# Rope scores of the last attention layer: made in a stage of their own, or as steps of the layer's own list

## The reference, cut to what matters

```
ckv = x @ Wkv;  kr = rope(ckv @ Wkr);  qr = rope(x @ Wqr)       # kr, qr: 2048 x 64
k, v, q = ckv @ Wkup, ckv @ Wvup, x @ Wq                        # 16 heads of 16
ar = qr @ kr.T                                                  # 2048 x 2048, one for all heads
scores = (q @ k.T + ar) / scale, causal;  out = softmax(scores) @ v @ Wo
```

## Time and profile before

| | |
|---|---|
| median of 3 runs | 2820.98 us |
| profiled execution | 2811.07 us, span 2809.3 us |
| PE busy | 2515.8 us, 90% |
| DVE busy | 1890.8 us, 67% |
| ACT busy | 1232.5 us, 44% |
| mean granted TensorE clock | 0.91 of full |

### The profile page before, as it was taken

The page is one execution under the profiler, slowest core; times in us unless marked ns, Lnnn a source line. Parts: engine busy times, 40 slices in busy tenths (PEclk is TensorE's granted clock), DMA queues, the critical chain, the costliest instruction groups (busy, mean ns, idle before and its releaser), DMA issues.

```text
span 2809.3 us, 38846 instructions
## 1 busy us (share of the span) xinstructions
PE 2515.8 (90%) x14390; PEld 1277.0 (45%) x14390; DVE 1890.8 (67%) x4599; ACT 1232.5 (44%) x1494; POOL 151.6 (5%) x338
## 2 busy tenths in 40 slices
PE   5899989989999998999999999987675999999985
PEld 3543434335555655433333333334333556565654
DVE  6466878844545442888888888764735777776618
ACT  3233656661111112166676667664110355555541
POOL 3100102110000000000000000000000001010100
PEclk9756999999999999599999999899875899999998
DMA  5600303000000004400300300000177326262200
GB/s 193 130 1 1 46 2 47 2 1 19 1 0 1 12 1 160 54 1 2 46 1 1 46 1 1 1 1 16 56 216 194 79 72 115 65 114 68 60 1 30
DMA packets 73905, 130.44 MB, mean 46 GB/s; under 512 B 12530, under 2 KB 31730, under 8 KB 70130
## 3 DMA queue, kind: packets, MB, share of 16 engines
q1 hardware_dynamic: 73716, 127.97, 20.4%
HBM read 88.84 MB, written 38.27 MB: 45 GB/s over the span
## 4 chain that ended last, share of the span: by engine, by line
PE 66%; DVE 21%; DMA 5%; issue 3%; SPq 3%; ACT 2%; POOL 0%; DVEq 0%; ACTq 0%; POOLq 0%
PE PS L971 18%; PE PS L888 15%; PE PS L742 12%; DVE MP L1324 11%; PE PS L748 7%; PE PS L950 7%; PE PS L846 4%; SPq L485 2%; ACT PF L1110 1%; DVE QF L1165 1%; PE PS L896 1%; DVE ST L1158 1%; DMA QR<-MRL 1%; DMA rope_scores<-HT 1%; DMA WA<-rope_scores 1%
## 5 line engine op out<-in xcount | busy, mean ns | idle before, releaser
L1110 ACT ACTIVATE PF<-PS 128x1024 f32<-128x1024 f32 (+3 forms) x1152 | 1055.1, 952 | 879.5 <-PE PS L950 525.7
L1324 DVE TENSOR_REDUCE MP<-PS 128x1 f32<-128x512 f32 (+3 forms) x1664 | 987.8, 652 | 217.2 <-PE PS L888 142.9
L888 PE MATMUL PS<-KR,QR 48*128 48x512 f32 (+3 forms) x2304 | 775.3, 481 | 107.4 <-DVE MP L1324 43.4
L888 PEld LDWEIGHTS PS<-KR,QR 48*128 48x128 f32 x2304 | 354.5, 202 | 652.4 <-DVE MP L1324 473.6
L971 PE MATMUL PS<-PF,VO 128*32 128x512 f32 (+3 forms) x4608 | 606.8, 601 | 0.2
L950 PE MATMUL PS<-QR,KR 50*128 50x512 f32 (+3 forms) x2304 | 510.0, 433 | 27.9 <-DMA QR<-MRL 21.2
L1320 DVE CUSTOM_DVE_ANT_0 JUNK<-PS,WA 128x512 bf16<-128x512 f32 (+3 forms) x512 | 286.5, 605 | 117.6 <-issue 48.9
L950 PEld LDWEIGHTS PS<-QR,KR 50*128 50x128 f32 x2304 | 248.9, 198 | 214.9 <-ACT PF L1110 139.7
L748 PE MATMUL PS<-RQ,RK 64*128 64x512 f32 (+3 forms) x1920 | 260.8, 371 | 0.0
L742 PE MATMUL PS<-HT,WA 128*128 128x512 f32 x512 | 221.1, 592 | 0.0
L696 POOL TENSOR_SCALAR_AFFINE_SELECT PF<-PF 128x256 f32<-128x256 f32 x256 | 103.7, 408 | 2165.4 <-ACT PF L1110 2162.3
(11 more groups left out here) (142 smaller groups left out, 1423.0 us busy)
## 6 DMA issues: line engine op xcount, KB each, us to landing
WA<-rope_scores SPq DMA_DIRECT2D x88, 256.0 KB, 3.2
rope_scores<-HT SPq DMA_DIRECT2D x28, 256.0 KB, 2.5
WC<-rope_scores SPq DMA_DIRECT2D x24, 256.0 KB, 3.2
QR<-parts_a_q SPq DMA_DIRECT2D x18, 256.0 KB, 7.7
KR<-parts_a_k SPq DMA_DIRECT2D x18, 256.0 KB, 10.2
QR<-parts_b_q SPq DMA_DIRECT2D x18, 256.0 KB, 12.8
KR<-parts_b_k SPq DMA_DIRECT2D x18, 256.0 KB, 16.4
QR<-parts_c_q SPq DMA_DIRECT2D x18, 256.0 KB, 7.0
```

The lines of the kernel that those rows point to most:

```text
L888: ins = mm(bank(slots[h][0], w), QR[rows, t0 + tb * P:t0 + (tb + 1) * P], KR[rows, t0 + s0:t0 + s0 + w], start=True, stop=not masked)
L1110: sc.activation(PT[:, u % SETS, 2 * q:2 * q + 2, off:CH], src, ACT.Exp).then_inc(L.exp_done, 1)
L1324: ins = v.reduce_max(MP[:, i, c, y:y + 1], src, AX.X)
```

## The change

The stage `ar` is taken out. A step `("rope", n)` stands in C's own list in front of the maxima of tile n, for group 0 alone, with a planner cost of 1.0 w / 512 + 0.3. It takes one bank of the ring of three: PE makes the three products, DVE moves the bank to `AR[n % 5]`, where the maxima of the next steps read it, waits for its own write (`ar_made`) and frees the bank; SP writes the tile to DRAM. From the sixth tile on DVE waits until the tile that lay in the buffer before is written out. Groups 1 to 3 read the tiles back as before. The first reads come at the end of group 0. SP loads the last rope chunk and the last stack chunk directly behind `p2`, and the stacks of group 1 in three pieces of four DMAs, behind the `pv` steps 0, 5 and 10.

```diff
@@ plan
+            if self.rope and g == 0 and p == 0:
+                ones.append((1.0 * w / CH + 0.3, ("rope", n // NP)))
             ones.append(((1.24 if self.rope else 1.14) * w / CH + (0.34 if self.rope else 0.1), ("max", n)))
-TAKES = {"max": 2, "mtr": 1, "otr": 1}
+TAKES = {"max": 2, "mtr": 1, "otr": 1, "rope": 1}
-                   ("", wave("o1", "hyp", "p2") + each("ar")), ("C", None), ("", wave("o2", "hypout"))]
+                   ("", wave("o1", "hyp", "p2")), ("C", None), ("", wave("o2", "hypout"))]
@@ SP, attention_steps
-                for g in range(2, NG):
+                for g in range(1, NG):
                     for i in range(3):
-                        stacks[(g - 1) * L.n_group - 1 + STACK_STEP * i] = (g, i)
+                        stacks[max(0, (g - 1) * L.n_group - 1) + STACK_STEP * i] = (g, i)
...
-                        if n < n_tiles:
+                        if len(L.tiles) <= n < n_tiles:
                             sp.wait_ge(L.slot_free, ring)
+                            if n - AR_RING < len(L.tiles):
+                                sp.wait_ge(ar_out[n % AR_RING], 16 * (n // AR_RING))
                             settled("sp", sp)
                             ar_load(L, n)
+                    if step[0] == "rope":
+                        n = step[1]
+                        tb, i, s0, w = L.tiles[n]
+                        sp.wait_ge(ar_made, n + 1)
+                        sp.dma_start(scr_ar[tb, :, s0:s0 + w], AR[n % AR_RING][:, 0:w]).then_inc(ar_out[n % AR_RING], 16)
@@ SP, attention
-                if not L.rope:
-                    parts_in_dram(L, NC - 1)
+                parts_in_dram(L, NC - 1)
+                if L.rope:
+                    load_rope(L, NC - 1)
                 load_chunk(L, NC - 1)
...
-                    for i in range(NC):
-                        sp.wait_ge(ar_out[i], 16 * ar_place.count(i))
-                    for n in range(AR_RING):
-                        ar_load(L, n)
-                sp.wait_ge(L.stack_in, NC * STACK_DMAS)
-                load_stacks(L, 1, 1)
@@ PE, attention
+                    if step[0] == "rope":
+                        tb, i, s0, w = L.tiles[step[1]]
+                        if tb % BPC == 0 and i == 0:
+                            pe.wait_ge(L.rope_in, (tb // BPC + 1) * ROPE_DMAS)
+                        for part in range(len(ROPE_PARTS)):
+                            ins = rope_product(bank(slot, w), step[1] % 2, RQ, tb * P, P, RK, s0, w, part)
+                        ins.then_inc(L.slot_ready, 1)
@@ DVE, attention_steps
+                    if step[0] == "rope":
+                        a = step[1]
+                        tb, i, s0, w = L.tiles[a]
+                        if a >= AR_RING:
+                            dve.wait_ge(ar_out[a % AR_RING], 16 * (a // AR_RING))
+                        dst, src = AR[a % AR_RING][:, 0:w], bank(slot, w)
+                        if s0 + w == (tb + 1) * P:
+                            v.tensor_tensor(dst, src, MASK[:, CH - w:CH], ALU.add).then_inc(ar_made, 1)
+                        else:
+                            v.tensor_copy(dst, src).then_inc(ar_made, 1)
+                        dve.wait_ge(ar_made, a + 1)
+                        dve.sem_inc(L.slot_free, 1)
                     if step[0] == "max":
...
-                        if L.rope and p == 0:
-                            dve.wait_ge(ar_in[a % AR_RING], 16 * (a // AR_RING + 1))
+                        if L.rope and p == 0 and g > 0:
+                            dve.wait_ge(ar_in[a % AR_RING], 16 * ((a - len(L.tiles)) // AR_RING + 1))
```

More of the change, by code:

```diff
@@ L309, in build @@
         AR = [WA[:, 4096 + CH * n:4096 + CH * (n + 1)] for n in range(4)] + [WC[:, 1792:2304]]
-        ARS = [HT[:, c].rearrange("p k t -> p (k t)") for c in range(NC)]
         NAT = {"gate": QF[:, 0:2048].rearrange("p (m d) -> p m d", d=D),
@@ L356, in build @@
         x_done = sem("x_done")
-        ar_out = [sem(f"ar_out{i}") for i in range(NC)]
+        ar_made = sem("ar_made")
+        ar_out = [sem(f"ar_out{i}") for i in range(AR_RING)]
         ar_in = [sem(f"ar_in{i}") for i in range(AR_RING)]
@@ L384, in build @@
                  "ffn": (18, 0), "lin": (6, 2), "hyp": (2, 0), "hypout": (2, 0)}
-        ar_banks = lambda c: (BPC * (c + 1), 0)
         D_COUNT, A_COUNT, HT_AT = {}, {}, []
@@ L395, in build @@
                 steps[i] = (k, c, d_total, a_total)
-                d_banks, a_banks = ar_banks(c) if k == "ar" else BANKS[k]
+                d_banks, a_banks = BANKS[k]
                 d_total += d_banks
@@ L408, in build @@
                     NORM_OF[k, c] = len(HT_AT)
[L411 to L414, removed]
         L_KEY = {"a": "A", "b": "B", "c": "C"}
@@ L535, in attention_steps @@
                         if i == 0:
-                            sp.wait_ge(L.pv_done, (g - 1) * L.n_group)
+                            if g > 1:
+                                sp.wait_ge(L.pv_done, (g - 1) * L.n_group)
                             sp.wait_ge(L.stack_in, (g - 1 + NC) * STACK_DMAS)
@@ L549, in load_rope, with attention @@
                         sp.dma_start(dst[HALF * h:HALF * (h + 1), i, t].bitcast(F32), scr_r[w][i, :, t]).then_inc(L.rope_in, 16)
-            def rope_tiles(L, c, d0):
-                if c == 0:
-                    parts_in_dram(L, NC - 1)
+            def attention(L):
+                parts_in_dram(L, NC - 1)
+                if L.rope:
                     load_rope(L, NC - 1)
[L556 to L562, removed]
-                if not L.rope:
-                    parts_in_dram(L, NC - 1)
                 load_chunk(L, NC - 1)
@@ L611, in _ @@
                         project(k, c, d0)
-                    if k == "ar":
-                        rope_tiles(L2, c, d0)
                     if k == "hypout":
@@ L854, in main @@
                     token_major(lambda kk, i: VH[:, kk, blk(i)], lambda kk: OUTW[k][:, kk, :], KD, d_bank, d_ready)
[L855 to L863, removed]
                 if k in ("hyp", "hypout"):
@@ L1244, in main @@
                         v.tensor_copy(NW[:, 6, 0:1], ONE[:]).then_inc(l1w_free, 1)
[L1245 to L1258, removed]
                 if k in ("hyp", "hypout"):
@@ L1300, in attention_steps @@
                 for step in L.steps:
-                    if step[0] in ("mtr", "otr"):
+                    if step[0] in ("mtr", "otr", "rope"):
                         n = ring.next()
@@ L1386, in attention @@
                     dve.wait_ge(a_free, A_COUNT[L_KEY[L.name]])
-                    for i in range(NC):
-                        dve.wait_ge(ar_out[i], 16 * ar_place.count(i))
                 attention_steps(L)
```

## The result

Before 2820.43 us, after 2786.02 us (medians of four runs each): ratio 0.988, interval 0.9848 to 0.9911, 34.4 us less where 27.4 were forecast. Timed again in a second series with more runs of the kernel before, the pair gave 2811.9 and 2791.8 us, ratio 0.9922, interval 0.9899 to 0.9944: some 20 to 22 us. The two series overlap only at the ends of their intervals. A likely reason is that the stages ahead of C vary from run to run: in the changed kernel's profile of the second series the last projection ends at 2108.6 us instead of 2087.6. How much of the difference between the medians that makes is not shown. One place where it shows is the middle of the kernel, at another granted clock.

A forecast was written before the change was run, and what follows sets the result against it. DVE, with the ring of three banks, was taken to pace group 0's maxima, PE all after; 49.4 + 14.7 - 29.7 - 4.0 - 3.0 = 27.4 us gained, 2821.0 - 27.4 = 2793.6 us; forecast's case 2781 to 2805 (0.70).

The forecast's parts named there:

- Start of C: End of p2: DVE starts at about 2090.8 instead of 2140.2, 49.4 us earlier, PE waiting only for p2's last banks.
- The pause: 2152.3 to 2167.0, DVE waiting for a tile read behind stack loads: 14.7 us go, as group 0 reads nothing back.
- Group 1's stacks at nothing: Three load pieces, about 9 us each, hidden by four tiles of slack; without cover up to 5 us a piece.
- DVE waits on the writes: Rival, chance 0.09: each stack piece holds tile writes and row DMAs back, 5 us each, 15 us lost, 2809.
- Rows of chunk 0, 3 us: First score near tile 6: PE waits for chunk 0's row DMAs behind four tile writes, DVE runs dry, 3 us.
- Own wait and increment, 4.0 us: Behind each of 40 moves: DVE's wait for its own write and the semaphore increment, 0.1 us each time.
- Moves at 24.3 / 0.82 = 29.7 us, products covered at nothing: Group 0: 40 moves on DVE, the pacing engine, 82% busy; PE's 25 us of products hidden behind DVE's time.
- The dear bound: All in place, products not covered: 64.1 - 24.3 - 4.0 - 25 - 3 = 7.8 us gained, 2813.
- series: Rival, chance 0.12: with three banks, rope product and move run one after the other in group 0; time 2813.
- The end moves by as much: After group 0's maxima, order and PE's pace stay, so the kernel's end moves as much as theirs.
- Slower by the clock: Rival, 0.05 with another wait: clock stays at 1.2 GHz through group 0, 53 us lost against 27 gained, 2847.
- up about 30 us behind it: Sign in the new profile: the clock rises about 30 us behind the first score, itself near 2115.

The follow-up runs named there:

- pieces alone: The kernel before, with only group 1's stacks loaded in three pieces behind pv 0, 5 and 10; ratio 0.9939 to the kernel before.
- four of the edits: Changed kernel with one rope product of three (0.9875), move freeing bank (0.9917), ACT making moves (0.9954), or rope step directly behind preceding first-pass step, move freeing bank (0.9944).

## Why the prediction was right, point by point

The time (2793.6 forecast, 2786.0 measured), the direction and the two large terms, 64.1 us gained at the start of C, were right. The price of the rope steps was not, and its mechanism was half wrong. The sum was 4.5 us too good for what the change does inside C (27.4 against 22.9). The 34.4 us of the first timing are some 11 us more than the profiles show inside C, and the second series gives 20 to 22; that the first came out on the good side of the forecast is luck.

- *Start of C*, 49.4 us earlier: 49.2. *The pause*, 14.7 us: gone; pieces alone give 15.1.
- *Group 1's stacks at nothing*: right. 9 us a piece, writes landing in up to 9.7 us, no wait. The rival "DVE waits on the writes" is what happens with whole stacks (24.7 us), and not in this change.
- *Rows of chunk 0, 3 us*: too dear. The first score's product starts at 2111.69 and no wait of DVE or PE in group 0 ends with a DMA.
- *Own wait and increment, 4.0 us*: too cheap for each move. The gap of the earlier trace rows prices the wait alone (0.11 us); the separate increment, put at nothing, is 0.22 more. The edit that took it away gave 3.0 us of the 8.8 that 40 times 0.22 would be, since behind other moves DVE waits for PE anyway.
- *Moves at 24.3 / 0.82 = 29.7 us, products covered at nothing*: the step that failed. It says that DVE paces and PE hides behind it. DVE idles 19.7 us for the products; two thirds of the product less give 12.5 us, half of the moves less only 6.9. The rope steps cost 41.5 us, 1.04 each, where moves and own waits were put at 33.7: 7.8 us too little, of which the 3 us for the rows, which did not come, hid a part. The dear bound, with the products in full, was 56.3 us. So the rival "series", which had 0.12, is half of what happened. That chunk 1 had not been slower at the half clock did not show that PE had room for three more products: its maxima are one product for each bank DVE empties, the rope step three.
- *The end moves by as much*: 22.4 us at the end of group 0, 22.9 at the end of the kernel. It holds only while the clock stays up behind group 0; in four of the edits it did not.
- *Slower by the clock*: did not come. The granted clock was up for the rest of group 0 from about 2149, 37 us behind the first score and 61 behind the end of p2 (some 113 before). It had been up for moments before that, the first time some 14 us behind the first score, and fell again; the forecast "up about 30 us behind it" has only the last rise. Windows of the changed kernel:

```profile
2126.00:2128.00 2.00, 1.44 (x14) 1.36 (x13) 2.00 (x7) 0.85 (x2) 0.41 (x1) 1.00 0.29 110
...
2140.00:2148.00 8.00, 7.57 (x34) 4.99 (x35) 3.96 (x18) 1.03 (x1) 0.00 (x0) 0.50 1.00 122
...
2150.00:2160.00 10.00, 8.96 (x68) 6.26 (x69) 7.82 (x27) 4.50 (x5) 0.00 (x0) 1.00 0.16 56
```

What stays open is why the clock dips in some orders and not in others.

## What to carry to other kernels

Look for a bulk load ahead of small transfers on one queue: here it stopped what the small ones feed. It shows as one long time to landing; cut the load up before restructuring anything: here that alone gave two thirds. Work put into a pipeline with few buffers can cost on both engines at each end of a buffer. Price it between the covered price and the sum, as here (33.7, 41.5 and 53.3 us, rows left out), and do not take the covered one unless the trace shows that the other engine has room. A gap read from rows prices only the instructions that stand in it; a semaphore increment of its own is one more. Compare versions from a mark just ahead of the changed stage when earlier stages vary by more than the effect.

## What the runs showed of the hardware

The stretch behind a common mark repeats to 0.1 us in two runs whose earlier stages differ by 21 us. The granted clock fell to a mean of 0.60 over 12.8 us in which PE was busy 11.8; the same instructions ran at 1.00 in a kernel whose group 0 was 3 us longer. Moving 24 us of copies from DVE, 75% busy, to ACT, 26% busy, made that stretch 12.1 us longer. Behind a 0.69 us move DVE's next operation started 0.25 us after the end when it waited for its own write and a separate increment stood between, 0.03 us after it with the wait alone, and 0.08 us before it with neither.
